# The layer norms' reciprocal square root as a power on GpSimd instead of nine VectorE steps

## What is computed

```python
mu = mean(x, axis=-1)
var = mean((x - mu) ** 2, axis=-1)
(x - mu) * rsqrt(var + 1e-5) * g + b
```

## Time and profile before

| | |
|---|---|
| median of three runs | 5544.78 us (5543.81 to 5547.71) |
| the profiled execution | 5542.44 us, its span 5540.8 us |
| PE busy | 90% of the span |
| DVE busy | 70% |
| ACT busy | 70% |
| POOL busy | 12% |

### The profile page before, as it was taken

How to read it: one execution, slowest core, us unless ns; L and a number is a source line. 1 busy time by engine, 2 the same in 40 slices (tenths; PEclk the granted TensorE clock), 3 DMA queues, 4 the chain that set the end, 5 groups by cost and what they waited for, 6 DMA issues and landing times.

```text
span 5540.8 us, 134688 instructions
## 1 busy us (share of the span) xinstructions
PE 5010.1 (90%) x43556; PEld 2901.0 (52%) x43556; DVE 3897.8 (70%) x7702; ACT 3868.6 (70%) x6261; POOL 647.0 (12%) x959
## 2 busy tenths in 40 slices
PE   5888889999999999999999999999999999868777
PEld 2444456666767666777666744433333333333343
DVE  4887888888988888988888855555555555444454
ACT  5888776888766888767888756677777777533333
POOL 0133100234000333000342000000000000000000
PEclk9998999999999999999999999999999999978888
DMA  1334468667687666787676743121111111000000
GB/s 63 133 140 141 140 182 240 230 228 236 222 230 233 227 229 230 237 232 246 220 233 227 230 129 86 57 60 54 46 54 51 46 54 54 13 4 4 8 7 5
DMA packets 398465, 756.32 MB, mean 137 GB/s; under 512 B 246065, under 2 KB 304818, under 8 KB 332602
## 3 DMA queue, kind: packets, MB, share of 16 engines
q1 hardware_dynamic: 378170, 704.04, 39.8%
q0 software_dynamic: 19968, 48.01, 3.7%
HBM read 397.49 MB, written 354.42 MB: 136 GB/s over the span
## 4 chain that ended last, share of the span: by engine, by line
PE 53%; DVE 16%; ACT 12%; issue 11%; SPq 4%; DMA 3%; ACTq 1%; DVEq 1%
PE ps_t L1027 8%; PE ps_y L921 7%; PE ps_t L933 5%; PE ps_f L1012 4%; PE ps_y L913 4%; PE ps_f L921 3%; DVE big L1344 3%; ACT big L1171 3%; DMA big<-hstore 3%; PE ps_t L942 3%; PE ps_t L1036 2%; ACT big L1180 2%; ACT big L1187 2%; SPq L730 2%; DVE big L1332 2%
## 5 line engine op out<-in xcount | busy, mean ns | idle before, releaser
L1351 DVE TENSOR_REDUCE big<-big 128x16 f32<-128x512 f32 x1280 | 844.5, 672 | 655.1 <-ACT big L1171 653.3
L1344 DVE TENSOR_TENSOR big<-big 128x512 f32<-128x512 f32 x1280 | 939.7, 765 | 30.3 <-DVE big L1373 18.8
L1171 ACT ACTIVATE big<-ps_y 128x512 f32<-128x512 f32 x892 | 544.7, 611 | 512.0 <-PE ps_y L921 458.8
L933 PE MATMUL ps_t<-ident,big 128*128 128x128 f32 x5120 | 801.3, 280 | 28.4 <-DVE big L1344 25.1
L1187 ACT ACTIVATE big<-ps_t,g_now 128x512 f32<-128x512 f32 x1024 | 816.8, 798 | 12.3 <-PE ps_t L933 11.7
L921 PEld LDWEIGHTS ps_y<-conv_now,big 128*128 128x128 f32 x5088 | 622.5, 193 | 364.3 <-issue 364.3
L1180 ACT ACTIVATE big<-ps_t 128x512 f32<-128x512 f32 x1024 | 628.2, 614 | 168.6 <-PE ps_s L958 103.7
L921 PE MATMUL ps_y<-conv_now,big 128*128 128x128 f32 x5088 | 723.4, 286 | 0.0
L942 PE MATMUL ps_t<-ident,big 128*128 128x128 f32 x4096 | 640.3, 280 | 89.9 <-ACT big L1180 88.1
L933 PEld LDWEIGHTS ps_t<-ident,big 128*128 128x128 f32 x5120 | 581.1, 143 | 264.2 <-issue 219.1
L942 PEld LDWEIGHTS ps_t<-ident,big 128*128 128x128 f32 x4096 | 475.1, 143 | 240.4 <-issue 143.2
(11 more groups left out here) (195 smaller groups left out, 7220.8 us busy)
## 6 DMA issues: line engine op xcount, KB each, us to landing
hstore<-big SPq DMA_DIRECT2D x256, 1024.0 KB, 4.1
big<-hstore SPq DMA_DIRECT2D x256, 1024.0 KB, 5.3
xmodes<-x_out SPq DMA_DIRECT2D x128, 312.0 KB, 4.4
y_kt<-ymodes SPq DMA_DIRECT2D x512, 78.0 KB
ymodes<-y_st SPq DMA_DIRECT2D x192, 144.0 KB, 2.5
ymodes<-y_st SPq DMA_DIRECT2D x64, 192.0 KB, 3.3
w_raw<-in_tok_w1r POOLq DMA_DIRECT2D x128, 72.0 KB, 4.3
w_raw<-in_tok_w2r POOLq DMA_DIRECT2D x128, 72.0 KB, 4.2
```

The lines of the kernel that those rows point to most:

```text
L933: last = nc.tensor.transpose(ps_t1[:, 128 * b:128 * b + 128], y_sb[2 * k + wh][:, 128 * b:128 * b + 128], ident[:, :])
L1171: af(y_sq[wh], of[:, wh, :], ACT.Square).then_inc(s["sq_done"], 1)
L1344: v_.tensor_tensor(groups(y_sb[2 * k + wh]), groups(y_sb[2 * k + wh]), rstd[:, k // 2, at:at + 16].unsqueeze(2).to_broadcast([128, 16, 32] ...
L1351: v_.tensor_reduce(ss[:, k // 2, at:at + 16], groups(y_sq[wh]), AX.X, ALU.add).then_inc(s["ss_done"], 1)
```

## The change

DVE's `rsqrt_half` is taken out with both places that call it. POOL gets a `rsqrt_half` of two instructions of 128x64: the mean of squares plus epsilon into `var`, and, after a wait for it (`var_done`), `var` to the power of a tile that holds -0.5. It stands at two places in POOL's `body`. Half 0 comes ahead of `order_x` in the stem and behind it in layers and head; half 1 comes at the end, behind both `add_weights`. `norm_step` now counts one for each half. `then` is a wait followed, where the value is a loop variable, by a no-operation.

```diff
+        half_power = sb("half_power", [128, 64])
...
+            nc.gpsimd.memset(half_power[:, :], -0.5)
...
+            def rsqrt_half(n, j):
+
+                then(pool, "ss_done", 8 * n + 4 * j + 4)
+                nc.gpsimd.tensor_scalar(var[:, :], ss[:, j, :], 1.0 / CH, EPS, ALU.mult, ALU.add).then_inc(s["var_done"], 1)
+                then(pool, "var_done", 2 * n + j + 1)
+                nc.gpsimd.tensor_tensor(rstd[:, j, :], var[:, :], half_power[:, :], ALU.pow).then_inc(s["norm_step"], 1)
...
+                if front == "stem":
+                    rsqrt_half(n, 0)
                 if back2 in STORED:
                     order_x(n - 2)
+                if front in MIXED:
+                    rsqrt_half(n, 0)
                 if slots is not None:
                     for second in range(2):
                         add_weights(ph, q - 8, slots[second], second)
+                if front is not None:
+                    rsqrt_half(n, 1)
...
-                dve.wait_ge(s["norm_step"], NEWTON * (half + 1))
+                dve.wait_ge(s["norm_step"], half + 1)
...
-            def rsqrt_half(n, j):
-
-                step, at, r, t, v = s["norm_step"], NEWTON * (2 * n + j), rstd[:, j, :], nt[:, :], var[:, :]
-                dve.wait_ge(s["ss_done"], 8 * n + 4 * j + 4)
...
-                    if k % 2 and front is not None:
-                        rsqrt_half(n, k // 2)
...
-                    if k == 0:
-                        rsqrt_half(n - 1, 1)
-                    if k == 2 and front is not None:
-                        rsqrt_half(n, 0)
```

More of the change, by code:

```diff
@@ L18 @@
 RUN = KX * CH
-NEWTON = 9
 D, E, H = 64, 8, 128
@@ L124, in vit_tower @@
             "h_loaded0", "h_loaded1", "h_stored0", "h_stored1", "y_loaded", "xmodes_stored", "ymodes_stored",
-            "y_done", "sq_done", "y_read", "ss_done", "norm_step", "xhat_done", "t1_done", "act_done", "t2_done",
+            "y_done", "sq_done", "y_read", "ss_done", "var_done", "norm_step", "xhat_done", "t1_done", "act_done", "t2_done",
             "px_done", "f_done", "tw_done", "fw_done", "fw_read", "xout_done", "iw_done", "iw_read",
```

## The result

The changed kernel takes 7997.2 us (median of 4 runs, 7996.6 to 7999.2) where the kernel before takes 5544.3 us: a ratio of 1.4426, 95% interval 1.4403 to 1.4448. The forecast was 5685 us with a range of 5440 to 6450 us. The direction was the one forecast; the size was far outside, 2453 us instead of 140.

A forecast was written before the change was run, and what follows sets the result against it. PE alone was taken to bound the head, latency the stem, PE with DVE close behind the layers; slot quads +55 and +48, other layer quads +46, stem -9, head 0 made +140 us, 5685 us, range 5440 to 6450.

The forecast's parts named there:

- P: Duration of one power on POOL, estimated at 3.0 us from twenty steps, with 0.3 and 6.1 us as ends.
- The third rival: Very slow power, 6.1 us, delays halves in layers and stem: +915 us, 6460 us; chance 0.08 for over 6 us.
- L = 0.75 + P: Latency from a half's last sum to its first `normed`: hand-overs and `tensor_scalar` 0.75 us plus the power, 3.75 us.
- The sum: Delays over all stretches at a 3.0 us power: +55, +48, +46, -9 and 0, together +140 us, 5685 us.
- Half 0 of the slot quads: In layers, the second product, still held by POOL's add, comes 1.0 us late for PE, x48 = +48 us.
- The stem: Transposes run beside POOL; half 0 takes 3.75 instead of 4.29 us, about 17 on the chain: -9 us.
- The head: Latency stays under 8.2 us of cover: 0; power over 7 us would cost each of 64 halves the excess.
- POOL's order: Half 1's power ahead of `load_raw` delays its loads, but margin stays about 1.1 us for any duration: nothing.
- The second place where both engines read SBUF: With the head, one `normed` beside the power would be held until it ends, about 3303.0; cost taken as 0.
- rival 1: Cheap power, up to 2.0 us, shortens slot quads and stem: 5463 us at 1.0, 5442 at 0.3; chance 0.40.
- the page's rule: GpSimd about two times slower than VectorE for two inputs; for the power that would mean 0.45 us, about 5450 us.
- the second rival: Balance: at latency about 3.0 us the slot quads' loss meets the stem's 34 us gain, 5545 us; chance 0.08.

The follow-up runs named there:

- filler66: Changed kernel with 66 identity transposes added on TensorE ahead of its wait for each half's first product in stem and layers; 7612.4 us, ratio 1.3747.
- pow16: Changed kernel with the power over 16 of 64 columns, the other 48 set to 1.0; 5752.2 us, ratio 1.038 to the kernel before.
- mult64: Changed kernel with the power replaced by a product of two constants, norm left out; 5476.3 us, ratio 0.9881 to the kernel before.
- headpow: Kernel before with the GpSimd power only in quads that run with the head, nine VectorE steps elsewhere; 5550.3 us, ratio 1.0013.

## Why the prediction was wrong

**The power's duration, the term that failed.** P was put at 3.0 us as twenty elementary steps of 0.15 us, with 6.1 us (forty steps) as the upper end. It is 10.56 us, 0.159 us for each element: by the prediction's own step of 2.4 ns an element, about 66 of them. The step price was read from a copy and an add, and neither says how many such steps a power takes or at what rate they run. No run shows of what steps a power is made; what the runs show is its duration at three widths. Nothing in the trace of before bounded that number from above; forty was a choice. The third rival, a very slow power, is what happened. Its chance of 0.08 for "P over 6" was far too small, and the range's upper end, 6450 us, rested on the forty steps. The 0.45 us that the prediction worked out for a GpSimd two times slower than VectorE is too short by a factor of 23, and the add itself, by the prediction's own figures, stands at 3.3 to 1.3 ns, 2.6 times.

**The hand-overs.** L = 0.75 + P was nearly right: 0.16 us from DVE to POOL, 0.24 for the `tensor_scalar`, 0.15 for POOL's wait on itself, 0.03 back, 0.58 + P in the run above. The term was 0.17 us too long, of no weight here.

**The sum, once P is known.** At L = 11.13 the prediction's terms are 48 x 8.5 = 409, 48 x 8.4 = 403, 96 x 7.7 = 739 and, in the stem, 32 x (6.8 + 7.4) = 457: 2008 us, without the head. Measured are 1933 + 509 = 2442. Of the 434 us that are missing, 389 are the clock (the changed kernel less filler66, in layers and stem). That mechanism stood nowhere in the prediction, though its view by stretch had a granted clock of 0.93 in the stem, where PE idles more. The remaining 45 us can be read in filler66, whose clock is up: its slot quads lost 852 us for the 812 of the sum, the other layer quads 776 for 739, and the stem 425 for 457. The other layer quads hid 0.75 us of each half's longer latency, where the sum let off 1 us. The slot quads hid nothing: 17.8 us each for two latencies that grew by 17.3. The knee lies near the latency of the kernel before, as pow16 and mult64 show from both sides.

**Half 0 of the slot quads.** Right in kind: in the changed kernel, too, the pair collides with the add, in all 48 quads, and keeps its 2.9 us. Its term was too small at the latency that was forecast. At 3.7 us a slot quad lost 2.96 us, where both latencies in full are 2.4 and the forecast's two terms 2.1. The second pair, which the add now holds as well, is a candidate for the rest; that was not tested.

**The stem.** Transposes and power do run side by side, and at 3.7 us the stretch is as long as before (-10 us forecast, 0 measured); with 8 to 9 us between runs of the same code the two cannot be told apart. The term itself was misread: of the 35 stem blocks on the chain 29 are half 0, not about 17, which would make it -16.

**The head.** Right that it costs nothing; wrong that each microsecond over 8.2 would. At 11.1 us of latency the stretch is 1537.0 against 1533.6 us, and headpow agrees.

**POOL's order.** Right for the changed kernel: ACT's L1220 waits for no transfer there, and mult64, with the same order, is faster than before. At the P that was forecast the margin is gone in the stem, where ACT waits at each slot quad of pow16; in the layers it holds there, too.

**The second place where both engines read SBUF.** Wrong, at no cost: the power was to hold a DVE product beside it, and the product took its 0.68 us. What grew instead is the hold by POOL's adds, from one pair to two in a slot quad.

**The gain of a cheap root (rival 1).** The mechanism is real, its size was over: 5442 us forecast for P = 0.3, 5476 measured. Of the 92 us that the rival had in the layers it kept 60%, 55 us, and 23 arrived; of the 79 us in the stem it kept 47, and 39 arrived. The prediction's words on the page's rule point at the second rival and mean this one.

## What to carry to other kernels

Counting instructions says nothing when the operation itself is new to the trace: measure the one instruction at two widths before moving nine others for it, and if that is not possible, let the range say that its duration is unknown. Where an engine's step lies between the last input and the first output of a tightly coupled loop, a microsecond more can cost a microsecond each time, as here, while a microsecond less may bring a tenth of it. If TensorE is what then waits, add the clock: here it made the loss 19% larger (389 us on 2064), and it can be separated by filling the wait with work that does nothing.

## What the runs showed of the hardware

- A power of two tensors on GpSimd (fp32, 128 partitions) took 2.91, 5.44 and 10.56 us for 16, 32 and 64 elements of a partition, 0.36 us and 0.159 us an element; a product in the same form took 0.32 us for 64.
- GpSimd's power did not hold VectorE's product with two inputs in SBUF (0.68 us beside it; 0.69 at most of 256 with the head), while GpSimd's add of 128x576 held both that product (the pair 2.95 us instead of 1.29) and a 128x64 step (1.87 us instead of 0.23). The Trainium skill (SBUF — State Buffer, section "Who interferes with whom") has the contention for any GpSimd instruction that reads SBUF; the add agrees, the power does not. Why it differs was not tried.
- TensorE's clock was at its lower level (matmuls of 1.75 and 1.94 us where filler66 has 0.97 and 1.16) behind idle stretches of 2.7 and 1.1 us with four transposes of 0.66 us together between them, and the granted clock of the slot quads was 1.00 when the first of these was filled with transposes of no use.
- GpSimd took 0.16 us to start behind VectorE, 0.15 us behind its own instruction, and VectorE 0.03 us behind GpSimd (changed kernel, at 2066).
